# The second passes of a gated state recurrence: the product of turned query and state is written for GpSimd instead of VectorE, for all tokens but the last

## The reference, cut to what matters

```
def step(Sc, inp):
    a11, a12, bt, k, v = inp
    S0, S1 = (Sc[..., 0], Sc[..., 1])
    r0 = a11[..., None] * S0 + a12[..., None] * S1
    r1 = -a12[..., None] * S0 + a11[..., None] * S1
    Sr = jnp.stack([r0, r1], -1)
    err = v - jnp.sum(k * Sr, -1)
    Sn = Sr + bt[..., None, None] * err[..., None] * k
    return (Sn, Sn)
...
_, Y = jax.lax.scan(step, S0, xs)
y = jnp.sum(Q * Y, -1).reshape(b, s, DI)
```

## Time and profile before

| | us |
|---|---|
| median of the three runs (lowest to highest) | 1590.58 (1589.28 to 1590.63) |
| the profiled execution, own time | 1591.3 |
| its span in the profile | 1589.2 |
| PE busy | 1275.8 |
| DVE busy | 1231.9 |
| ACT busy | 425.5 |
| POOL busy | 142.9 |
| 32 products, L1417, DVE | 39.0 |
| 32 sums, L901, POOL | 75.9 |

### The profile page before, as it was taken

One profiled execution on the slowest core, in us unless ns is written; L12 is line 12 of the kernel. 1 busy time (PEld: TensorE's weight loads), 2 busy tenths in 40 slices (PEclk: granted clock), 3 DMA queues, 4 the chain that ended last, 5 costly groups with the idle time before them and its releaser, 6 DMA issues. The chain is left out here.

```text
span 1589.2 us, 12623 instructions
## 1 busy us (share of the span) xinstructions
PE 1275.8 (80%) x4244; PEld 747.0 (47%) x4244; DVE 1231.9 (78%) x1980; ACT 425.5 (27%) x645; POOL 142.9 (9%) x64
## 2 busy tenths in 40 slices
PE   2980777733988769498599999899988695999997
PEld 1540333322545446245366666565544363666664
DVE  4799999998999976869989999977999866330111
ACT  2443101000001133453533232230011343432332
POOL 0000112110212200000001111101212100000000
PEclk9995899976999889789799999999999897999999
DMA  4000011010211121300023222303111100623221
GB/s 159 1 7 0 40 53 44 36 53 0 93 53 40 40 111 54 113 0 7 14 95 97 98 94 67 106 33 126 53 53 40 53 1 6 217 75 124 80 80 66
DMA packets 52112, 98.69 MB, mean 62 GB/s; under 512 B 4689, under 2 KB 40018, under 8 KB 50898
## 3 DMA queue, kind: packets, MB, share of 16 engines
q1 hardware_dynamic: 52050, 97.91, 17.5%
HBM read 75.87 MB, written 22.02 MB: 62 GB/s over the span
## 5 line engine op out<-in xcount | busy, mean ns | idle before, releaser
L635 PE MATMUL ps<-kz 128*128 128x256 f32 x1024 | 243.8, 381 | 14.2 <-ACT kz L836 12.5
L621 PE MATMUL ps<-kz 128*128 128x512 f32 x512 | 245.4, 603 | 6.2 <-DVE coef L1026 4.1
L635 PEld LDWEIGHTS ps<-kz 128*128 128x128 f32 x1024 | 195.2, 191 | 96.8 <-issue 60.7
L527 PE MATMUL ps<-wshare,uT 128*128 128x512 f32 x512 | 230.1, 603 | 0.0
L836 ACT ACTIVATE kz<-ps,small 128x512 f32<-128x512 f32 x128 | 87.6, 686 | 303.5 <-PE ps L621 303.2
L458 PE MATMUL ps<-wshare,xnT 128*128 128x512 f32 x256 | 119.1, 609 | 56.1 <-ACT ps L699 56.1
L527 PEld LDWEIGHTS ps<-wshare,uT 128*128 128x128 f32 x512 | 96.7, 194 | 110.4 <-issue 110.4
L621 PEld LDWEIGHTS ps<-kz 128*128 128x128 f32 x512 | 99.2, 194 | 84.6 <-issue 74.5
L890 POOL TENSOR_TENSOR work<-work 128x1024 f32<-128x1024 f32 x28 | 66.8, 2387 | 710.9 <-DVE work L1313 412.4
L768 ACT ACTIVATE kz<-ps 128x512 f32<-128x512 f32 x32 | 19.1, 597 | 358.2 <-PE ps L512 358.2
L1573 DVE TENSOR_TENSOR kz<-ps,b_s 128x256 f32<-128x256 f32 x16 | 6.3, 413 | 135.9 <-PE ps L635 135.9
(11 more groups left out here) (263 smaller groups left out, 1933.1 us busy)
## 6 DMA issues: line engine op xcount, KB each, us to landing
kz<-in_w SPq DMA_DIRECT2D x128, 256.0 KB, 3.0
kap_d<-kz SPq DMA_DIRECT2D x26, 512.0 KB, 2.7
kz<-kap_d SPq DMA_DIRECT2D x26, 512.0 KB, 3.2
uT<-in_x SPq DMA_DIRECT2D x8, 512.0 KB, 5.4
wshare<-in_wq SPq DMA_DIRECT2D x2, 2048.0 KB, 7.8
kz<-in_x SPq DMA_DIRECT2D x2, 2048.0 KB, 7.9
coef<-in_x SPq DMA_DIRECT2D x2, 2048.0 KB, 7.8
wshare<-in_wk SPq DMA_DIRECT2D x2, 1024.0 KB, 11.2
```

Source lines behind the costliest of these rows:

```text
L527: t = mm(ps[:, 2 * (j % 2) + c, :], uT3[:, k, j * P:(j + 1) * P], wq_s[:, k, c, :], start=(k == 0), stop=(k == KI - 1))
L621: t = mm(ps[:, 4 + i % 2, :], w1_r[r][:, k, (f % 2) * P:(f % 2 + 1) * P], x2T[:, k, n * 512:(n + 1) * 512], start=(k == 0), stop=(k == KM ...
L635: t = mm(ps[:, 6 + q // 2, (q % 2) * DM:(q % 2 + 1) * DM], hbuf(i)[:, q * P:(q + 1) * P], w2_r[r][:, f % 2, :], start=(f == 0 and q % 2 == ...
```

## The change

The product of token j (j = 0 to 14) leaves DVE's list and enters POOL's, behind the sum of token j. POOL's product waits for its own sum (`turned_ready`) and for the new semaphore `stt_ready`, which is released by the state's sum `st` = `sr` + `Y` of token j. It releases `yp_ready` as the product did before. Since POOL now reads `st`, DVE's sum of token j waits for `yp_ready` of token j-1 before it overwrites `st`. The dependency of L1428 on the state goes through `stt_ready` instead of DVE's chain semaphore. The product of token 15 stays on DVE, and POOL only waits there.

```
--- before.py
+++ after.py
@@ -212,6 +212,7 @@
         ym_ready = sem("ym_ready")
         turned_ready = sem("turned_ready")
         yp_ready = sem("yp_ready")
+        stt_ready = sem("stt_ready")
         yt_ready = sem("yt_ready")
         yt_done = sem("yt_done")
         gq_ready = sem("gq_ready")
@@ -888,6 +889,7 @@
                     if i >= 2:
                         pool.wait_ge(sum_ready, b * (L - 2) + i - 1)
                     nc.gpsimd.tensor_tensor(PSt[:, :, 2], PSt[:, :, 2], Z, ALU.add).then_inc(sum_ready, 1)
+                st = work[:, 0:1024].rearrange("p (i n) -> p i n", i=2)
                 if b > 0:
                     pool.wait_ge(d_done, b * NF)
                 for j in range(L):
@@ -899,6 +901,10 @@
                     w = [bass.AP(w.tensor, w.offset + 512 * a, [list(w.ap[0]), [3072 if j % 2 else 1024, 2], [1, 512]])
                          for a in range(2)]
                     nc.gpsimd.tensor_tensor(qb(j), w[0], w[1], ALU.add).then_inc(turned_ready, 1)
+                    pool.wait_ge(turned_ready, b * L + j + 1)
+                    pool.wait_ge(stt_ready, b * L + j + 1)
+                    if j < L - 1:
+                        nc.gpsimd.tensor_tensor(qb(j), qb(j), st, ALU.mult).then_inc(yp_ready, 1)
 
 
         @block.vector
@@ -1424,11 +1430,10 @@
                 at["st"] = n_chain[0]
                 for j in range(L):
                     k = k2(j)
-                    after(at["st"])
+                    if j == 0:
+                        after(at["st"])
                     mark(tt(by_head(sr[:, 0], 0), by_head(st[:, 0], 0), wide(cf[:, RHO, j]), MUL))
                     at["sr"] = mark(tt(by_head(sr[:, 1], 0), by_head(st[:, 1], 0), wide(cf[:, RHO, j]), MUL))
-                    if j >= 1:
-                        product(j - 1)
                     if j >= 3:
                         dve.wait_ge(k_loaded[j % KR2], k_loaded_count(b, j))
                     after(at["sr"])
@@ -1448,8 +1453,10 @@
                     after(at["e"])
                     tt(Y, k, e.unsqueeze(1).to_broadcast([P, 2, DI]), MUL).then_inc(k2_used, 1)
                     dve.wait_ge(k2_used, b * L + j + 1)
-                    at["st"] = mark(tt(st, sr, Y, ADD))
-                after(at["st"])
+                    if j >= 1:
+                        dve.wait_ge(yp_ready, b * L + j)
+                    tt(st, sr, Y, ADD).then_inc(stt_ready, 1)
+                    dve.wait_ge(stt_ready, b * L + j + 1)
                 product(L - 1)
                 dve.wait_ge(yp_ready, b * L + L)
                 group_stats(b, NCH - 2)
```

## The result

The changed kernel takes 1624.82 us (median of four runs, 1624.45 to 1625.39) against 1589.93 us of the kernel before (four runs, 1588.99 to 1590.63). The ratio is 1.0220 with a 95% interval of 1.0202 to 1.0238: it is 34.9 us slower. The forecast was 1623.0 us with a range of 1600 to 1632, and the measured time lies in it. The span of the profiled execution went from 1589.2 to 1623.0 us.

A forecast was written before the change was run, and what follows sets the result against it. DVE was taken to bound the second passes, at 10.36 us a token against PE's 9.09. POOL's hold on the port outweighs the 1.01 us gain, netting +1.08 us a token: 1590.6 + 32.4 = 1623.0 us, range 1600 to 1632.

The forecast's parts named there:

- DVE sets the pace and its loss reaches the end: Second passes: DVE takes 10.36 us a token, PE needs 9.09; DVE's difference carries in full to the program's end.
- The gain of 1.01 us a token: From L1429 to L1435, DVE takes 1.73 us with the product and 0.72 without; 30 products move, 30.3 us.
- POOL's product takes as long as its sum: The moved multiplication on POOL was taken at 2.35 us, the median of POOL's additions of the same size.
- The rival of a dear product: POOL's product takes longer than a sum: 1641 us at 2.9 us, 1693 us at 4.7 us; chance 0.07.
- The added waits cost nothing: New waits of DVE and POOL are covered; instructions with two waits start 0.03 us after the one they depend on.
- The port holds one until the other is done: POOL and DVE instructions with two SBUF inputs block each other for a whole instruction; DVE lost 2.03 to 2.04 us.
- The rival without a hold: POOL's product runs freely beside L1428, L1429 and L1435; only the 30.3 us gain stays: 1560.3 us; chance 0.06.
- the one in which POOL waits for the turn: POOL's product gets the port only after L1435, beside the two L1412: +0.36 us a token, 1601.4 us; chance 0.10.
- the one in which POOL comes ahead of L1428: POOL's product takes the port before the first half of `sr`: +1.29 us a token, 1629.3 us; chance 0.05.
- Which gap POOL takes: Where after the state's sum DVE lets the port go to POOL's product; left open, +1.08 us a token taken.
- two cases: POOL gets the port between L1429 and L1435, +1.02 us a token, or between L1428 and L1429, +1.14 us.
- The signs: Expected profile: POOL's products recorded with 2.8 to 3.4 us, token about 11.4 us, DVE's busy time +24 us.

The follow-up runs named there:

- the last experiment: Kernel before with the next value scaled ahead of the component sum, plus token 15's turned-parts sum made by DVE instead of POOL: 1584.92 us, ratio 0.9981.

## Why the prediction was right, point by point

- *DVE sets the pace and its loss reaches the end.* Shown: the passes grew by 18.39 + 17.94 = 36.3 us. The pieces ahead of, between and behind them moved by -0.5, -1.2 and -0.8 us, no more than they do in the other kernels, and the span grew by 33.8 us.
- *The gain of 1.01 us a token.* Shown, less two small terms: in the kernel without the product a steady token takes 10.36 - 9.54 = 0.82 us less. Of the missing 0.19 us, 0.07 are the wait for the keys from token 3 on (below) and 0.12 POOL's later start in that kernel.
- *POOL's product takes as long as its sum.* Shown: 2.36 us beside the turn. The rival of a dear product falls.
- *The added waits cost nothing.* Right for `yp_ready` and `stt_ready`: L1458 and L1435 start 0.03 to 0.04 us after the instruction ahead, as before. Missed for a wait that wasn't touched: with the product gone, the wait for the loaded keys lies open and costs 0.07 us in 26 tokens, 1.8 us. I had taken the gap of token 0, which has no such wait, for all tokens.
- *The port holds one until the other is done.* Shown from four sides: the held line, its absence without the product, its move with the product's place, and its scaling with the product's length. The rule of the Trainium skill ("SBUF — State Buffer", section "Who interferes with whom"), an exclusive hold of the shared interface for the whole instruction, agrees with all four. The rival without a hold, and the one in which POOL waits for the turn, fall with L1436's 2.83 us; the one in which POOL comes ahead of L1428 falls with L1435's 0.69 us.
- *Which gap POOL takes.* I left two cases open and took the middle, +1.08 us. It was the dearer one, +1.14 us: POOL gets in between L1435 and L1436, although these two overlap in the records. With the 0.07 us of the keys' wait that makes 1.21 us, and 11.56 - 10.36 = 1.20 us was measured. This one choice and the keys' wait make up 30 x 0.06 + 1.8 = 3.6 us, the difference between the 32.4 us forecast and the 36.3 us by which the passes grew, but for 0.3 us. The whole program lost a little less than the passes, 34.9 us by the runs.
- *The closeness of 1623.0 to 1624.82.* In part luck. The forecast change was 32.4 us and 34.9 us were measured; 0.7 us of the difference is hidden because the forecast started from 1590.6 us, the median of three runs, and the median of four is 1589.93. The passes missed by 3.9 us, and the pieces around them, which nobody forecast to move, took 2.5 us back in the profile.
- *The signs.* The products on POOL are recorded with 2.78 to 2.79 us, one of the 30 with 2.45, just under the 2.8 to 3.4 us named, since they wait for L1435 and not for L1436. DVE's busy time grew by 1264.8 - 1231.9 = 32.9 us and not by 24. The forecast took the product's full 1.22 us off, but in the busy time stretches in which two instructions overlap count once, and the product overlapped by 0.08 and 0.09 us with its neighbours, so only 1.05 us go; and the hold is 2.15 us instead of 2.03. 30 x (2.15 - 1.05) = 33 us.

## What to carry to other kernels

Before moving an elementwise operation from DVE to POOL, look at what DVE runs in the stretch in which the moved one will run. Here it was free beside DVE instructions that read PSUM, which kept their 1.22 us. Beside DVE instructions with two SBUF inputs, DVE paid nearly POOL's whole duration: 2.15 us of 2.36, for a product that cost DVE 1.01 us. An instruction that is now and then much longer than its line's median is worth a look before any change is made: the 2724 ns in a line of 676 was such a hold, as the last experiment shows. When an instruction leaves a gap that it used to fill, look at every wait that sits in that gap, in the steady tokens and not in the first one.

## What I had not expected of the hardware

POOL's waiting instruction gets in between two DVE instructions that overlap by 0.08 us in the records and have no dependency between them: all 30 times it was L1436 that stood still, and never L1440. In all 30, POOL's record starts behind L1435's start and ahead of L1436's. It makes no difference how long ahead: POOL starts 0.50 us before L1436 in 29 of them and 0.16 us before it in one (492.55 to 492.71 in batch 0), and the hold is 2.83 us there too.

The wait for the loaded keys ahead of L1440 costs 0.07 us (0.11 instead of 0.04 us) when nothing covers it. Not every second wait does so: L1445 before has two in token 15 and started 0.03 us after the line it depends on, L1458 has two and starts 0.03 us after the one ahead, and so does L1437 in the experiment that moved the keys' wait there. At these three places the wait that ends last stands first in the program; at L1440 it stands behind the keys' wait. No run swaps the two, so that this order is what sets them apart is not shown.
